# Expert slots of 32 rows in four column tiles, with sixteen weight homes, in a fused GNN and mixture-of-experts kernel

## The reference, cut to what matters

```python
scores = jax.nn.sigmoid(x @ router_w.T);  biased = scores + bias_corr
# the best 4 of 8 groups of experts, and in these the best K = 6 experts by `biased`
w = scores[topk] / (scores[topk].sum(1) + 1e-20)
g = einsum('sc,ech->seh', x, Wg)      # (625, 64, 160): Wg, Wu are (64, 512, 160)
u = einsum('sc,ech->seh', x, Wu)
routed = einsum('seh,ehc->sc', combine[:, :, None] * silu(g) * u, Wd)    # Wd is (64, 160, 512)
out = shared + routed                 # shared: a dense silu-gated layer of 512
```

## Time and profile before

| | us |
|---|---|
| Median of 3 runs | 2492.97 |
| Profiled execution | 2492.98 |
| Its span | 2491.2 |
| PE busy | 2335.4 (94%) |
| ACT busy | 717.6 (29%) |
| Block of the 61 steps | about 1834 to 2093 |

### The profile page before, as it was taken

How to read it: one execution, slowest core, us unless ns; L and a number is a source line. 1 busy time by engine, 2 the same in 40 slices (tenths; PEclk the granted TensorE clock), 3 DMA queues, 4 the chain that set the end, 5 groups by cost and what they waited for, 6 DMA issues and landing times. The chain is left out here.

```text
span 2491.2 us, 33816 instructions
## 1 busy us (share of the span) xinstructions
PE 2335.4 (94%) x11401; PEld 1509.1 (61%) x11401; DVE 1126.0 (45%) x2712; ACT 717.6 (29%) x1398; POOL 649.4 (26%) x652
## 2 busy tenths in 40 slices
PE   5898969999999999999999999999989998889998
PEld 4475547757757765466576576576644444457775
DVE  8733985545545546735344344253623333530002
ACT  0422333323343322225134144153212221112211
POOL 0563666506506510000101101001124542101110
PEclk9898989999999998999999999999989998979999
DMA  3122026517507523020110110010056553558885
GB/s 90 49 72 72 1 84 213 147 31 232 150 28 228 152 69 112 17 81 1 58 60 22 37 60 23 34 51 13 18 174 230 176 187 116 123 201 306 319 292 194
DMA packets 73533, 281.58 MB, mean 113 GB/s; under 512 B 22298, under 2 KB 22426, under 8 KB 65438
## 3 DMA queue, kind: packets, MB, share of 16 engines
q1 hardware_dynamic: 38363, 188.09, 22.1%
q0 software_dynamic: 35008, 91.33, 12.4%
HBM read 354.71 MB, written 30.43 MB: 155 GB/s over the span
## 5 line engine op out<-in xcount | busy, mean ns | idle before, releaser
L86 PE MATMUL ps<-XT,W 128*128 128x250 f32 (+1 forms) x1200 | 334.6, 434 | 3.5 <-ACT XT L1420 1.6
L86 PEld LDWEIGHTS ps<-XT,W 128*128 128x128 f32 x1200 | 228.5, 193 | 106.1 <-issue 21.7
L1150 PE MATMUL ps<-XN,W 128*128 128x512 f32 x498 | 256.7, 598 | 2.6 <-ACT GT L1472 2.6
L1856 POOL TENSOR_TENSOR H<-H,RB 125x512 f32<-125x512 f32 x40 | 50.6, 1267 | 724.0 <-DVE XN L2179 611.6
L2706 PE MATMUL ps<-W,HT 128*64 128x320 f32 x976 | 146.2, 442 | 4.7 <-issue 4.7
L2563 POOL DMA_INDIRECT result_rows<-KT,LOGC x77 | 78.3, 1017 | 260.5 <-DVE KT L3292 212.7
L86 PE MATMUL ps<-W,HT 128*128 128x512 f32 (+1 forms) x312 | 139.9, 602 | 0.8 <-ACT HT L3261 0.5
L86 PEld LDWEIGHTS ps<-HT,W 128*128 128x128 f32 x1088 | 126.5, 195 | 8.8 <-issue 7.7
L86 PE MATMUL ps<-HT,W 128*128 128x128 f32 x1088 | 126.7, 278 | 0.8 <-DVE HT L3272 0.8
L1126 POOL DMA_INDIRECT XT<-node_rows,LOGC x81 | 77.1, 952 | 173.8 <-DMA node_rows<-V 122.3
L1288 PEld LDWEIGHTS ps<-P,QT 128*128 128x128 f32 x672 | 89.2, 194 | 44.4 <-issue 44.4
(11 more groups left out here) (618 smaller groups left out, 4175.4 us busy)
## 6 DMA issues: line engine op xcount, KB each, us to landing
W<-in_L_ffn_Wgud SPq DMA_DIRECT2D x122, 896.0 KB
W<-in_L_ffn_w SPq DMA_DIRECT2D x36, 2048.0 KB, 7.8
W<-in_L_gnn_Wqkv SPq DMA_DIRECT2D x4, 3072.0 KB, 9.9
W<-in_L_gnn_W SPq DMA_DIRECT2D x5, 2048.0 KB, 14.9
W<-in_L_gnn_Wm SPq DMA_DIRECT2D x4, 2048.0 KB, 7.7
W<-in_L_ffn_Wd_rest SPq DMA_DIRECT2D x122, 64.0 KB
W<-result_rows SPq DMA_DIRECT2D x5, 1344.0 KB
RB<-in_L_gnn_rows SPq DMA_DIRECT2D x24, 256.0 KB, 4.2
```

The source lines that it names most:

```text
L86: last = nc.tensor.matmul(out, lhs(k), rhs(k), start=(k == 0), stop=(k == nk - 1))
L1150: nc.tensor.matmul(b.ps[:, n % PR, :], b.EAT[:, t * 128:(t + 1) * 128], We[layer], start=True, stop=True)\
L1856: ins = nc.gpsimd.tensor_tensor(b.H[0:R, t, :], b.H[0:R, t, :], b.RB[0:R, at:at + D], ALU.add)
```

## The change

Slots hold 32 rows instead of 64. A step has four slots in four column tiles, so still 128 rows. The worst case is 180 slots, which is 45 steps instead of 61. On the reference's inputs 132 slots have rows. There are sixteen homes of weights, four for each step modulo 4. They lie in `b.W` and in buffers that are free at that time. The same order of slots gives 39 real fetches out of 180, of which 12 are for steps 0 to 3; by step they are 3 3 3 3 1 1 0 1 1 0 0 1 1 2 0 0 1 1 2 0 1 0 1 1 0 1 1 1 1 0 0 0 0 0 0 1 2 0 1 0 0 0 1 1 2.

The rest rows of Wd have one home for each slot of a group of four steps, are now fetched only where the expert changes, and are issued by ACT: after the Silu of steps 4g+1 and 4g+2, for two steps each time. ACT waits before them until rest_down of the group before is done.

The gathers run 6 steps ahead instead of 8. SP reads its table for each step (one load of 8 registers), and the first five DMAs of the block go to its end: W1 after down(41), the others after down(43). The memsets and the tables of the block before are changed to fit.

```diff
-    WR, RR, GR, GU, early = 8, 2, 8, KD * 320, 2
-    CHAINS = WR // 2
+    WR, GR, GU, early = 4, 6, KD * 320, 2
...
+        homes = [(b.W, 7168), (b.W, 8960), (b.W, 10752), (b.W, 12544),
+                 (hf, 0), (b.W, 14336), (b.W, 0), (b.W, 1792),
+                 (xn, 0), (vf, 0), (pf, 0), (b.W, 3584),
+                 (xt, 0), (lf, 1024), (ht, 2880), (b.W, 5376)]
...
+    def read_rest_step(self, act, u):
+        act.load(self.rest_registers, self.steps[0:1, 8 * u:8 * u + 8])
+        return [act.snap(x, min_val=0, max_val=self.ne - 1 if i < 4 else 1) for i, x in enumerate(self.rest_registers)]
...
+    def load_rest(self, sp, u, j, step):
+        q = 32 * (u % 4)
+        sp.dma_start(self.w_rest[j][q:q + 32, :], self.weights("L2_ffn_Wd_rest", step[j]), cond=step[4 + j])\
+            .then_inc(self.rest_in[u // 4 % 2], 16)
...
         @block.sync
         def _(sp):
+            steps = [r.read_step(sp, u) for u in range(WR)]
+            for u in range(r.early, WR):
+                for j in range(4):
+                    r.load_main(sp, u, j, steps[u])
+            clear_retired(sp, retired)
+            for u in range(WR, NU):
+                steps.append(r.read_step(sp, u))
+                sp.wait_ge(s["d_mm"], u - WR + 1)
+                for j in range(4):
+                    r.load_main(sp, u, j, steps[u])
+            sp.wait_ge(s["d_mm"], NU - 3)
             sp.dma_start(W1[:, :], A["L3_gnn_W12"][:, 0:2048]).then_inc(p.g3_weights, 16)
+            sp.wait_ge(s["d_mm"], NU - 1)
             sp.dma_start(W2[:, :], A["L3_gnn_W12"][:, 2048:4096]).then_inc(p.g3_weights, 16)
...
                 for k in range(KD):
-                    for h in range(2):
-                        last = nc.tensor.matmul(b.ps[HALF[h], 1 + u % 2, 0:2 * HE], xT[u % 2][:, k, HALF[h]],
-                                                Wgu[(2 * u + h) % WR][:, k, :], start=(k == 0), stop=(k == KD - 1),
-                                                tile_position=(0, 64 * h))
+                    for j in range(4):
+                        last = nc.tensor.matmul(b.ps[QUARTER[j], 1 + u % 2, 0:2 * HE], xT[u % 2][:, k, QUARTER[j]],
+                                                Wgu[4 * (u % WR) + j][:, k, :], start=(k == 0), stop=(k == KD - 1),
+                                                tile_position=(0, 32 * j))
...
+            def rest_in(first, n):
+                for v in range(first, min(first + n, NU)):
+                    if v >= 4:
+                        act.wait_ge(s["y_mm"], 4 * (v // 4))
+                    step = r.read_rest_step(act, v)
+                    for j in range(4):
+                        r.load_rest(act, v, j, step)
...
                 nc.scalar.activation(sil[u % 2], b.ps[:, 1 + u % 2, 0:HE], ACT.Silu).then_inc(s["silu"], 1)
+                if u == 0:
+                    rest_in(0, 2)
+                elif u == 1:
+                    rest_in(2, 2)
+                elif u % 4 == 1:
+                    rest_in(u - 1, 2)
+                elif u % 4 == 2 and u > 2:
+                    rest_in(u, 2)
+            rest_in(NU - 1, 1)
...
-                    dve.wait_ge(s["y_mm"], 4 * (q // 4) + members(q // 4))
+                    dve.wait_ge(s["y_mm"], q + 1)
...
-    for i, (ne, k, ns, size) in enumerate(((64, 6, 61, 64), (8, 2, 17, 128))):
+    for i, (ne, k, ns, size) in enumerate(((64, 6, 45, 32), (8, 2, 17, 128))):
```

More of the change, by code:

```diff
@@ L2277, in l2_experts_block @@
     r.w_in = p.sems(*(f"f2_w_in{u}" for u in range(r.WR)))
-    r.rest_in = p.sems(*(f"f2_rest_in{u}" for u in range(r.RR)))
+    r.rest_in = p.sems(*(f"f2_rest_in{u}" for u in range(2)))
     r.arrived = p.sems(*(f"f2_rows_in{u}" for u in range(r.GR)))
@@ L2354, in _ @@
             pool.wait_ge(s["node"], 1)
[L2355 removed]
+            nc.gpsimd.memset(r.in_rows[4], 0.0).then_inc(s["cleared"], 1)
+            pool.wait_ge(s["cleared"], 7)
             for sl in range(r.GR):
@@ L2586, in read_steps @@
-    def read_steps(self, sp, at, n):
-        kept = []
-        for i, table in enumerate(self.steps):
-            regs = [self.step_registers[i][j] for j in range(n)]
-            sp.load(regs, table[0:1, at:at + n])
-            kept.append([sp.snap(x, min_val=0, max_val=self.ne - 1 if i == 0 else 1) for x in regs])
-        return kept
-    def load_weights(self, sp, u, h, e, new, used):
-        home, q = (2 * u + h) % self.WR, 32 * (u % 4)
-        sp.dma_start(self.w_all[home], self.weights("L2_ffn_Wgud", e), cond=new).then_inc(self.w_in[home], 16)
-        sp.dma_start(self.w_rest[u // 4 % self.RR][q:q + 32, 512 * h:512 * (h + 1)], self.weights("L2_ffn_Wd_rest", e),
-                     cond=used).then_inc(self.rest_in[u // 4 % self.RR], 16)
+        xn, hf, vf = (x[:, :, :].rearrange("p t n -> p (t n)") for x in (b.XN, b.H, b.V))
@@ new lines, in read_step, with load_main @@
+    def read_step(self, sp, u):
+        regs = self.step_registers[u % 4]
+        sp.load(regs, self.steps[0:1, 8 * u:8 * u + 8])
+        return [sp.snap(x, min_val=0, max_val=self.ne - 1 if i < 4 else 1) for i, x in enumerate(regs)]
+    def load_main(self, sp, u, j, step):
+        home = 4 * (u % self.WR) + j
+        sp.dma_start(self.w_all[home], self.weights("L2_ffn_Wgud", step[j]), cond=step[4 + j])\
+            .then_inc(self.w_in[u % self.WR], 16)
+    def load_rest(self, sp, u, j, step):
+        q = 32 * (u % 4)
+        sp.dma_start(self.w_rest[j][q:q + 32, :], self.weights("L2_ffn_Wd_rest", step[j]), cond=step[4 + j])\
+            .then_inc(self.rest_in[u // 4 % 2], 16)
@@ L2645, in l2_routed_blocks @@
     restT = [ht[:, 2624 + 128 * i:2752 + 128 * i] for i in range(2)]
-    HALF = (slice(0, 64), slice(64, 128))
+    QUARTER = [slice(32 * j, 32 * j + 32) for j in range(4)]
     def members(g):
@@ L2699, in gate_up @@
                 pe.wait_ge(s["xt_ready"], u + 1)
-                for h in range(2):
-                    pe.wait_ge(w_in[(2 * u + h) % WR], 16 * ((2 * u + h) // WR + 1))
+                pe.wait_ge(w_in[u % WR], 64 * (u // WR + 1))
                 if u >= 2:
@@ L2729, in down @@
                     pe.wait_ge(s["copied"], u - 3)
-                for h in range(2):
-                    last = nc.tensor.matmul(b.ps[HALF[h], 4 + u % 4, :], hT[u % 4][:, HALF[h]],
-                                            r.w_down[(2 * u + h) % WR], start=True, stop=False, tile_position=(0, 64 * h))
+                for j in range(4):
+                    last = nc.tensor.matmul(b.ps[QUARTER[j], 4 + u % 4, :], hT[u % 4][:, QUARTER[j]],
+                                            r.w_down[4 * (u % WR) + j], start=True, stop=False, tile_position=(0, 32 * j))
                 last.then_inc(s["d_mm"], 1)
```

121 lines of the change are left out of this document (57 added, 64 removed).

## The result

The kernel after takes **2460.40 us**, the median of 4 runs (2457.53 to 2462.23); before took 2494.11 beside it (4 runs, 2492.96 to 2495.43). The ratio is 0.9863, 95% interval 0.9851 to 0.9875: 33.7 us faster. The forecast was 2469, so 8.6 us of gain were missing in it; the range and the likeliest case's own range hold the result.

The account below looks back on a forecast made before the run. PE's work bounds the steady part, so the number of steps sets the time. Terms -66.3 + 2 + 8 + 1 + 29.5 + 1 + 1 = -23.8 from 2492.98 gave 2469 us, range 2443 to 2506.

Parts of the forecast that it names:

- the steps that go: In the block's steady part: 61 - 45 = 16 steps fewer at 4.145 us each, -66.3 us, if a step costs the same.
- ACT's bursts: Two-step bursts of DMA issues on ACT, 4.8 us each, stall PE 2.95 us a group, ten groups: +29.5 us.
- Four column tiles: In gate_up and rest_down: tiles of different columns overlap, 13 ns more a step and 0.1 us a rest_down group: +2 us.
- Rival C: In gate_up and down: four column tiles run only two at a time, doubling both; 2584 us; chance 0.05.
- Rivals A: On ACT: DMA issues cost little, a burst near 3.3 us, a group loses next to nothing; 2447 us; chance 0.15.
- B (over 21): On ACT: issues cost more, 6.6 us a burst, and the kernel is slower; 2505 us; chance 0.16.
- The formula: In a group of four steps: PE loses 2B - 6.65 us, B being a burst's length; 2.95 us at B = 4.8.
- The burst pays for itself nowhere: On ACT: moving the rest rows' issues there brings nothing, as SP had time, some microseconds of wait in each step.
- The start: In steps 0 to 3: more fetches delay gate_up(3) by 6.5, a lower-clock restart adds 1.4: +8 us; table loop +1.
- Weights in the steps: In later steps: fetches are nearly late where two follow on one (steps 13, 18, 36): +1 us.
- Rival D: In the steps: the weights bind, with waits at each pair of fetches, 10 more us; 2479 us; chance 0.07.
- The tail: At the block's end: last rest rows come some 4 us late, DVE's copies fall into that wait: +1, up to 4 us.

## Why the prediction was right, and where it was off

The forecast named the two mechanisms that set the time, the steps that go and ACT's bursts. Its first size was right and its second 10.8 us too large. The sum is nearer than that, since the other terms were 3.9 us too small, which is luck.

**The steps that go, -66.3.** Right. A step without a stall takes 3.84 to 4.93 us as before, and 40 steps without bursts' and weights' stalls took 165.9 us against 165.5.

**Four column tiles, +2.** It was at most 0.4 us, in the 40 steps of the run without weight fetches. Rival C is out. The 6 ns for a tile more were right; nothing waits for them, as the next four tiles follow after the 0.27 us that a pair took.

**ACT's bursts, +29.5.** The mechanism was right: two bursts in series, in the third and fourth step of a group, seen in the rows and by a slope of 1.9 where the formula has 2. Rivals A (groups of 16.6 us) and B (over 21) are out. The size was off: 18.7 us (21.5 with the waits for weights that they cover). In the group shown the bursts, from the start of the first read to the end of the last issue, were 4.66 and 4.76 us, not 4.8. And from Silu(u) to hidden_transposed(u+2), the first behind both bursts, were 1885.97 - 1874.97 = 11.00 us, so 1.58 us beside the two bursts where I had 2.2. The formula let the second burst begin when rows_out and Silu(u+1) had run; its first read began at 1879.84, 0.11 us after rows_out had started. 11.00 - 8.85 = 2.15 us a group, not 2.95 (the 11.00 are 10.1 to 11.5 over the ten groups). This is the largest error: 10.8 us too much, against 3.9 us that the other terms were too small together (16.9 for 13: start 10.3, weights and tiles 2.8, tail 3.8).

One link of the path was wrong. The forecast had PE wait for rows_out behind the first burst and for Silu and the products, in front of hidden_transposed, behind the second. In the trace rows_out, in front of rows_transposed, ends 19 of the 20 waits, behind both bursts. It cost the sum little, as hidden_transposed comes 0.52 us behind rows_transposed (1885.45, 1885.97). The 3 us between the spans' 30.7 and the medians' 33.7 are scatter: the profiled execution of after was the slowest of its four. SP's prices for issue and read held on ACT.

**"The burst pays for itself nowhere".** Right in this order of work, by the run with the rest rows on SP. But my reason that SP had time isn't the whole: what limits the split is when the rest rows are issued against the weights.

**The start, +8 and +1.** Measured +10.3: gate_up(3) begins 8.0 us later than before, for a forecast of 6.5 and 1 for the table, and the step behind it, at the lower clock, takes 2.3 us more, for a forecast of 1.4. The near hit hides two wrong readings. I took the first two bursts as hidden by the wait for weights ("nothing"): rows_transposed waits 2.79 and 1.71 us behind them, and the later start for the rest rows brings gate_up(3) some 3 us forward. And the weights moved at 394 GB/s up to 1850 and at 325 behind it, 355 over both, where I had 338.

In this trace rows_transposed(0) is 3.3 us later than before (1837.38, 1834.09), ahead of anything that the steps do. The table loop is 0.4 us of it (13.42 us for 13.03). 1.5 are `down` of the shared layer, which runs at the lower clock for longer behind it (0.53 and 0.94 in the same stretch; after first, then before):

```profile
1816.00:1822.00 6.00, 6.00 (x16) 2.56 (x9) 0.58 (x3) 0.00 (x0) 3.62 (x4) 0.53 0.69 257
```

```profile
1816.00:1822.00 6.00, 6.00 (x14) 2.58 (x13) 0.69 (x1) 0.00 (x0) 4.68 (x5) 0.94 0.29 77
```

The change alone doesn't make the clock stay low there: in the second trace of the same kernel it rose as early behind the loop as before, and from the loop to rows_transposed(0) were 20.1 us, as before (20.2), and not 21.7. Of the eleven traces with the new slots three have 20.0 to 20.1, and eight 21.4 to 21.7; why is open. The remaining 1.4 lie ahead of the loop, whose start varies by 2.7 us over the traces of the changed kernels. And little of it counts: that second trace won 2.2 us at gate_up(0) and 0.3 at gate_up(4).

**Weights in the steps, +1.** 2.8 us when nothing covers them, hidden in after. Rival D is out.

**The tail, +1, up to 4.** The table has +3.8, but the place to measure is the next layer's first matmul, 15.4 us behind the last gate_up instead of 10.8: +4.6, above the upper end. 2.7 are the late last rest rows. DVE's four copies do fall into that wait (they begin at 2059.80); the fifth doesn't. The other 1.9 us stay when the rest rows come early. There the last copy waits for a scatter, while W2 and the tables behind it, which the change moved to this place, are in flight. The forecast put this move at nothing. That these transfers slow the scatter is argued, and no run isolates it.

## What to carry to other kernels

An engine's DMA issues are work on that engine: 0.35 us each even if nothing moves, 0.75 for a read of 8 registers from a table. Count them into the chain through the busiest engine, and multiply by the number of bursts in series. Split them into portions that fit between two of the engine's deadlines (here portions of up to 3.6 us cost PE next to nothing, bursts of 4.7 us did), and issue small transfers early enough that a large one in front of them matters less: the same portions one step later took 182.2 us for the stretch instead of 171.5.

## What was not expected of the hardware

- A 64 KB DMA issued 0.9 us behind one of 0.92 MB on another engine's queue let its reader start only 5.6 us later. Separate issuers were no protection. The Trainium skill (DMA: Bandwidth & Descriptors, "Issuing engines are not separate DMA queues") says that DMAs of all issuing engines share the same 16 engines; the trace agrees, with these 5.6 us.
- PE's pauses of 0.9 us left the granted clock at 1.00; behind the pause that ends in 1.86 us of idle before rows_transposed it was 0.59, then 0.50, for some 4 us. A longer stall can be paid twice, unless the next stall covers the slow work. Its length doesn't settle it: the 4.38 us before gate_up(3) in after were followed by 0.50, 3.62 us at the same place in the run of three portions by 1.00.
- A second read with the same operands never reached the engine.
